# A Mamba block with a soft-tree FFN on one core: delta from eight rows of one product, and the leaf stages of the last group moved

## What is computed

```python
mod = (silu(c) @ wmod).reshape(2, 6, 1, 128)          # sa, ca, ga, sb, cb, gb; |ga|, |gb| at least 0.25
h = layernorm(x) * (1 + ca) + sa                      # x: (2, 2048, 128)
xp, z = split(h @ W_in)                               # 256 channels each
u = silu(causal_depthwise_conv(xp) + conv_b)
dt_r, Bm, Cm = split(u @ W_xp, [8, 24])               # 8, 16 and 16 columns
delta = softplus(dt_r @ W_dt + dt_bias)
h_t = exp(delta_t * A) * h_{t-1} + delta_t * B_t * u_t     # for each of 256 channels and 16 states
y_t = sum_n h_t[n] * C_t[n] + u_t * D_skip
x = x + ga * ((y * silu(z)) @ W_out)
h = layernorm(x) * (1 + cb) + sb
gate = sigmoid(h @ Wq.T @ routers.T)                  # 255 nodes of a binary tree
x = x + gb * (leaf_prob(gate) @ leaf_values @ Wout.T + Wout_b)
```

## Time and profile before

| | us |
|---|---|
| median of 3 runs | 494.55 |
| lowest, highest | 493.66, 495.66 |
| profiled execution, its own time | 495.33 |
| its span, first to last instruction | 493.5 |
| VectorE busy | 447.3 |
| GpSimd busy | 422.7 |
| TensorE busy | 406.7 |
| ScalarE busy | 378.1 |
| first scan starts | 29.64 |
| last scan ends | 471.4 |

### The profile page before, as it was taken

How to read it: one execution, slowest core, us unless ns; L and a number is a source line. 1 busy time by engine, 2 the same in 40 slices (tenths; PEclk the granted TensorE clock), 3 DMA queues, 4 the chain that set the end, 5 groups by cost and what they waited for, 6 DMA issues and landing times. The chain is left out here.

```text
span 493.5 us, 6708 instructions
## 1 busy us (share of the span) xinstructions
PE 406.7 (82%) x2133; PEld 279.7 (57%) x2164; DVE 447.3 (91%) x539; ACT 378.1 (77%) x690; POOL 422.7 (86%) x236
## 2 busy tenths in 40 slices
PE   7969665997499698997799788996899697687796
PEld 3537444675358456674558556664658455565474
DVE  6698899979999899989999889988999889999852
ACT  4478975598867898698967898698966898687715
POOL 6159899999999789998999899988999789999810
PEclk9999987997889989998999999998999989599799
DMA  6673045200830028300742027300741027300001
GB/s 168 160 298 151 1 144 222 87 0 1 301 126 27 0 42 327 108 0 2 248 149 77 2 66 303 106 2 0 259 156 60 1 62 306 107 2 21 0 1 43
DMA packets 24146, 51.06 MB, mean 103 GB/s; under 512 B 4521, under 2 KB 14256, under 8 KB 20016
## 3 DMA queue, kind: packets, MB, share of 16 engines
q1 hardware_dynamic: 24112, 50.64, 30.1%
HBM read 48.01 MB, written 2.62 MB: 103 GB/s over the span
## 5 line engine op out<-in xcount | busy, mean ns | idle before, releaser
L606 POOL TENSOR_TENSOR hc<-h,c_rows 128x1024 f32<-128x1024 f32 x127 | 298.4, 2366 | 27.0 <-DVE h L1382 26.3
L1382 DVE TENSOR_TENSOR_SCAN h<-dA,state,dbu 128x512 f32<-128x512 f32 x192 | 234.2, 1266 | 13.2 <-ACT dA L697 13.2
L697 ACT ACTIVATE dA<-delta,a_neg 128x512 f32<-128x512 f32 x256 | 173.2, 685 | 45.3 <-DVE h L1382 44.9
L1123 PE MATMUL yb<-ident,hc 128*128 128x128 f32 x1024 | 155.1, 287 | 17.8 <-POOL hc L606 16.6
L1123 PEld LDWEIGHTS yb<-ident,hc 128*128 128x128 f32 x1024 | 131.0, 149 | 64.9 <-issue 45.0
L1395 DVE TENSOR_TENSOR dbu<-du,bb 128x1024 f32<-128x1024 f32 x88 | 105.5, 1199 | 3.7 <-PE bb L1148 2.0
L593 POOL TENSOR_TENSOR dbu<-du,b_rows 128x1024 f32<-128x1024 f32 x40 | 94.6, 2364 | 4.1 <-DMA b_rows<-bc_dram 4.1
L1382 DVE TENSOR_TENSOR_SCAN h<-dA,dbu 128x512 f32<-128x512 f32 x64 | 74.2, 1205 | 5.5 <-ACT dA L697 5.4
L1023 PE MATMUL mf<-f_hT,w_conv 128*128 128x512 f32 x112 | 54.6, 612 | 2.0 <-ACT zu L757 1.4
L1148 PE MATMUL bb<-b_parts,sel 128*128 128x512 bf16 x63 | 25.1, 399 | 37.7 <-DVE dbu L1395 36.4
L1148 PEld LDWEIGHTS bb<-b_parts,sel 128*128 128x128 bf16 x88 | 8.6, 98 | 56.5 <-DVE dbu L1395 36.9
(11 more groups left out here) (206 smaller groups left out, 524.2 us busy)
## 6 DMA issues: line engine op xcount, KB each, us to landing
c_rows<-bc_dram SPq DMA_DIRECT2D x32, 1024.0 KB, 7.5
b_rows<-bc_dram SPq DMA_DIRECT2D x40, 256.0 KB, 8.9
xs<-in_L_attn_x_dram SPq DMA_DIRECT2D x8, 256.0 KB, 3.6
out_dram<-xs SPq DMA_DIRECT2D x7, 256.0 KB, 5.6
ygT<-in_L_attn_conv_w_dram SPq DMA_DIRECT2D x2, 256.0 KB, 4.3
bc_dram<-xd SPq DMA_DIRECT2D x8, 64.0 KB, 1.6
w_in<-in_L_attn_W_in_dram SPq DMA_DIRECT2D x2, 128.0 KB, 4.2
probT<-in_L_wmod_dram SPq DMA_DIRECT2D x1, 256.0 KB, 4.2
```

The costliest lines, as they stand in the source:

```text
L606: nc.gpsimd.tensor_tensor(hc[:, pair % RC, :, :], h[:, pair % RH, :, :], c_rows[:, q, n % NQ, :].unsqueeze(1).broadcast_to([P, HALVES, T]) ...
L697: nc.scalar.activation(dA[ke % RD][:, :], delta[:, ge % 2, half, :], ACT.Exp, scale=a_neg[:, half, n:n + 1]).then_inc(s_dA, 1)
L1123: last = nc.tensor.matmul(bank[:, tile], hc[:, pair % RC, half, tile], ident[:, :], start=False, stop=n == N - 1, is_transpose=True, skip_ ...
L1382: v.tensor_tensor_scan(h[:, pair % RH, half, :], dA[k % RD][:, :], dbu[:, pair % RW, half, :], start, ALU.mult, ALU.add).then_inc(s_scan, 1)
```

## The change

First, delta. The folded matrix `w_xdt`, its two transposes, two products and two copies go. W_xp's first eight columns stand in the product `xd` as rows 32 to 39 (`DT_ROW`), so `xd` gives dt, B and C in one product of two matmuls, now at steps 11 and 12. ScalarE copies it at step 13, and delta is one matmul for each half over the eight rows, at steps 14 (f) and 15 (t). Since the bank is then reused, a new product `br` at step 18 (the copy times the identity) puts `xd` back for the B parts. DRAM store and broadcast loads follow the copy.

In the first group the xd product's first half stands in front of the gate products, and four keep-warm matmuls are added, two of them while TensorE waits for the copy.

Second, the last group. Leaf stages of group 5 go to the front side's bank, at steps 4, 6 and 8 to 9 (`LAST_F`). Group 6's are `tr` 17, `node` 19 and 21, Softplus 23, `lp` 25 and 27, `ff` 29 and 30, which takes it out of `last_group`. Statistics, rstd, offset and normalisation of group 6 move from 14, 16, 16, 17 to 13, 14, 14, 15.

```diff
-              ("dt", 0): (1, (11, 12)), ("xd", 0): (1, (18, 19)), ("tr", 0): (2, (28,))},
+              ("xd", 0): (1, (11, 12)), ("dt", 0): (1, (14,)), ("br", 0): (1, (18,)), ("tr", 0): (2, (28,))},
-    ... ("dt", 1): (1, (13, 14)),
+    ... ("dt", 1): (1, (15,)),
...
-    LAST_SP = {2: -2, 25: -1}
+    LAST_F = (("lp", 0, -2, (4,)), ("lp", 1, -2, (6,)), ("ff", 0, -2, (8, 9)))
+    LAST_SP = {2: -2, 23: -1}
-    LAST_RSTD, LAST_OFF, LAST_XHAT = 16, 16, 17
+    LAST_STATS, LAST_RSTD, LAST_OFF, LAST_XHAT = 13, 14, 14, 15
...
             def dt_product(half):
-                for hh in range(HALVES):
-                    last = nc.tensor.matmul(yb[half][:, :], w_xdt[:, hh, half * P:(half + 1) * P],
-                                            zu[:, 0, HALVES + hh, :], start=hh == 0, stop=hh == HALVES - 1)
-                last.then_inc(s_dt0, 1)
+                nc.tensor.matmul(yb[half][:, :], w_dt[DT_ROW:DT_ROW + R, half * P:(half + 1) * P],
+                                 xd[DT_ROW:DT_ROW + R, :], start=True, stop=True).then_inc(s_dt0, 1)
...
                 elif name == "dt":
-                    if piece == 0:
-                        pe.wait_ge(s_silu, g + 1)
-                        if (side, g) == ("t", 1):
-                            pe.wait_ge(s_wtake, 1)
-                    last = nc.tensor.matmul(bank[:, :], w_xdt[:, piece, part * P:(part + 1) * P],
-                                            zu[:, g % 2, HALVES + piece, :],
-                                            start=piece == 0, stop=piece == HALVES - 1)
+                    wait_read(pe, "f", "xd", 0, g)
+                    if (side, g) == ("t", 1):
+                        pe.wait_ge(s_wtake, 1)
+                    last = nc.tensor.matmul(bank[:, :], w_dt[DT_ROW:DT_ROW + R, part * P:(part + 1) * P],
+                                            xd[DT_ROW:DT_ROW + R, :], start=True, stop=True)
+                elif name == "br":
+                    last = nc.tensor.matmul(bank[:, :], ident[:, :], xd[:, :], start=True, stop=True)
```

More of the change, by code:

```diff
@@ L69, in bass_adaln_mamba_tree_ffn_kernel @@
     NQ = N // QUARTERS
-    B_HI, C_ROW, B_MID, B_LO = 0, N, 64, 96
+    B_HI, C_ROW, DT_ROW, B_MID, B_LO = 0, N, 32, 64, 96
     PAIRS = K // HALVES
@@ L128, in bass_adaln_mamba_tree_ffn_kernel, with leaf_side @@
                     read_at[side].append(len(read_at[side]) + 1)
+    def leaf_side(g):
+        return "f" if g == GROUPS - 3 else "t"
     def due(name, part, g, s):
-        return [g + off for n2, p2, off, steps in jobs_of("t", g)
-                if (n2, p2, steps[-1] + 1) == (name, part, s) and ("t", name, part, g + off) in job_at]
+        side = "f" if g == LAST and name in ("lp", "ff") and any(job[0] == name and s == job[3][-1] + 1 for job in LAST_F) else "t"
+        return [g + off for n2, p2, off, steps in jobs_of(side, g)
+                if (n2, p2, steps[-1] + 1) == (name, part, s) and (side, name, part, g + off) in job_at]
     def softplus_due(g, s):
@@ L426, in _ @@
             sp.wait_ge(s_wz, 1)
-            for row, first, width in ((B_HI, R, N), (C_ROW, R + N, N), (B_MID, R, N), (B_LO, R, N)):
+            for row, first, width in ((B_HI, R, N), (C_ROW, R + N, N), (DT_ROW, 0, R), (B_MID, R, N), (B_LO, R, N)):
                 load(w_xp[:, :, row:row + width], xp_v[:, :, first:first + width], s_wxp)
@@ L901, in gate_products @@
                 last.then_inc(s_gatep, 1)
-            def dt_weight_transposes():
-                pe.wait_ge(s_wdtl, 16 * n_dt)
-                for hh in range(HALVES):
-                    last = nc.tensor.transpose(bb[0][0:R, hh * P:(hh + 1) * P], w_dtin[:, hh, :], ident[:, :])
-                last.then_inc(s_wdtt, 1)
-            def dt_weight_products():
-                pe.wait_ge(s_wdtc, 1)
-                for hh in range(HALVES):
-                    last = nc.tensor.matmul(dA[0][:, hh * DI:(hh + 1) * DI], w_dtin_t[:, hh * P:(hh + 1) * P],
-                                            w_dt[:, :], start=True, stop=True)
-                last.then_inc(s_wdtp, 1)
             def turn_x(bank, done):
@@ L961, in first_group @@
                                  skip_group_check=True).then_inc(s_r1, 1)
+                pe.wait_ge(s_wdtl, 16 * n_dt)
+                pe.wait_ge(s_modc, 1)
+                dt_product(0)
                 pe.wait_ge(s_gatec, 1)
                 dt_product(1)
+                pe.wait_ge(s_mid, 1)
+                nc.tensor.matmul(mb["f"][0][:, :], neg_ident[:, :], b_parts[:, 0, :], start=False, stop=True,
+                                 skip_group_check=True).then_inc(s_r2, 1)
                 pe.wait_ge(s_fxh, 2)
@@ L966, in first_group @@
                 turn_x(mb["t"][0], s_tr1)
-                pe.wait_ge(s_mid, 1)
-                nc.tensor.matmul(mb["f"][0][:, :], neg_ident[:, :], b_parts[:, 0, :], start=False, stop=True,
-                                 skip_group_check=True).then_inc(s_r2, 1)
             def weight_transposes(part):
@@ L1083, in product @@
                     if piece == 0:
-                        wait_read(pe, "t", "lp", 1, g)
+                        wait_read(pe, side, "lp", 1, g)
                         if g == 0:
@@ L1183, in last_group @@
                 y_sum(K - 5)
+                wait_read(pe, "f", "ff", 0, t - 2)
                 hold_rows(0)
-                product(t - 1, "t", "ff", 0, 0, 2)
                 for ks in range(K - 4, K):
@@ L1208, in last_group @@
                     last.then_inc(s_out7, 1)
-                product(t - 1, "t", "ff", 0, 1, 2)
+                keep_warm_on(dA[1], 1)
                 for i in range(2):
@@ L1413, in _ @@
                                         ALU.mult).then_inc(s_gate, 1)
-                    if tail and s == T_STATS:
+                    if tail and s == (LAST_STATS if g == LAST else T_STATS):
                         wait_read(dve, "t", "out", 0, t)
```

91 lines of the change are left out of this document (37 added, 54 removed), and 2 rows, old and new, of the table JOBS.

## The result

| | before | changed |
|---|---|---|
| median, us | 494.55 (9 runs) | 497.24 (9 runs) |
| lowest to highest | 492.86 to 495.66 | 493.84 to 498.86 |
| ratio of the changed kernel to before | | 1.0055, 95% interval 1.0029 to 1.0080 |

It is 2.7 us slower, where 2.5 us faster was forecast. The profiled execution of the changed kernel was its fastest (493.84, span 492.1); the other eight took 495.89 to 498.86.

The account below looks back on a forecast made before the run. The prediction took VectorE's scans (91% busy) as setting the pace. Start 2.0, middle 0.2 and last group 0.5 (less 3.7, plus 1.2 and 3.0) summed to 2.7 gained; against 494.55 it said 492.0 us, range 489.2 to 494.8.

Parts of the forecast that it names:

- The start, 2.0 gained: Up to the first scan: folded-matrix products gone, delta and gate instruction sooner; first scan at 27.3 instead of 29.64, 2.0 us booked.
- twice the time in low clock: Start, delta's two products: upper bound on their time, beside 0.86 us each as forecast.
- if the clock or a late transfer eats part: Start: low end of the gain, 0.7 us instead of 2.0.
- The middle, 0.2 gained: Middle groups: fewer products and xd's copy moved to step 13 without a wait; 0.2 us, between 1 lost and 1 gained.
- The last group, cost 3.7: Last group: early leaf sums and product delay yg's transpositions and the Silu block; step 13's decay at 444.3, not 440.59.
- uninterrupted work brings the clock back sooner: Last group, early leaf stages: full TensorE clock about 2 us sooner, saving about 1.9 us on the same queue.
- 1.2 back behind Softplus: Last group: group 6's Softplus at step 23 is covered by two dbu products; 1.2 of the 1.42 us stall returns.
- 3.0 back before `yg`: Last group: group 6's leaf product ends before the last sums, so the 3.48 us wait shrinks to within 0.5.
- The tail, nothing: Behind yg: the other half of group 6's leaf product and ScalarE's copy lay in waits, so removing them gains nothing.
- The low clock lasts through the early leaf stages: Rival, last group: leaf stages, transpositions and out product at half speed before the Silu block; 498 us, chance 0.08.
- The rule that the prediction took from the Trainium skill: Last group, between leaf stages: transposes do not count as TensorE work for the clock, so that stretch would lose it.
- The start does not carry: Rival, start: B's broadcast rows land when transfers allow, so only 0.7 us remains; 493.7 us, chance 0.17.

Follow-up runs that it names:

- e13: Changed kernel with the old last group, w_dt zeroed and loaded later, delta's products still over eight rows: 494.51 us, 1.0001 of the kernel before.
- e14: Changed kernel with the old last group, 128 rows in the first group's two delta products, eight in the other fourteen: 490.94 us, 0.9926 of before.
- e4: Changed kernel with five keep-warm matmuls instead of one between output product and last normalised rows' transpositions: 496.61 us, 1.0030 of before.
- e7: Changed kernel with group 5's leaf stages at steps 12, 14 and 16 to 17 instead of 4, 6 and 8 to 9: 492.65 us, 0.9956 of before.
- e10: Changed kernel with the old last group, all delta products over 128 rows, w_dt zero-padded and loaded later: 493.15 us, 0.9960 of before.
- e5: Changed kernel with the old last group and seven keep-warm matmuls instead of two during the wait for xd's copy: 494.13 us, 0.9992 of before.
- e6: Changed kernel with seven keep-warm matmuls instead of two while TensorE waits for xd's copy: 495.12 us, 1.0019 of before.
- e12: Changed kernel with group 5's leaf stages at 12, 14, 16 to 17 and seven keep-warm matmuls at the start: 492.36 us, 0.9959 of before.

## Why the prediction was wrong

**The start, 2.0 gained: the term was right and did not reach the end.** First scan forecast 27.3; ten profiles with eight rows have 27.02 to 28.44 (mean 27.8), the four with the old delta 29.54 to 30.58 (mean 30.0): 2.2 sooner. Its parts held: the gate TENSOR_SCALAR alone at 0.43, delta's products at the price of full ones. What failed is "I book 2.0 us", that a first scan started sooner is a kernel ended sooner. In nine of the ten the clock then stood at 1.2 GHz for 6.8 to 10.2 us, and 27.4 to 27.8 us passed to the Silu scan instead of 24.1 to 25.8. The low clock at the start had a place only as a bound ("twice the time in low clock" for delta's products, 0.7 "if the clock or a late transfer eats part"), and always on the way to the first scan; what TensorE does behind it, the z products and B fills, had no term. By e13 and e14 the cause is the eight-row form, which I had priced by its duration alone. Why a product over eight rows lets the clock fall, no run shows.

**The middle, 0.2 gained:** nothing; 372.3 to 372.6 in all but two profiles, both of the old delta (373.45, 373.94). The stalls behind the two table blocks are unchanged (1.53 behind Silu, 1.45 behind Softplus), ScalarE does not wait at the copy of `xd`.

**The last group, cost 3.7:** measured 3.1 to 4.4. Right in size and place: the sums at low clock in front of `yg` (2.05 and 1.91 for the first), the product in front of the fills. The gap before the scan of step 13 came as several stalls, not one. The hope that uninterrupted work brings the clock back sooner came true (426.4 in the first profile against 432.2 before), and the cost came all the same.

**The last group, 1.2 back behind Softplus:** 1.43 to 0.30, right.

**The last group, 3.0 back before `yg`: this is the mis-sized term.** It was read from 3.48 in the earlier trace rows as if every execution had it. The low clock that went with it, seen in the earlier trace rows, was that execution's; in before's second profile the wait is 1.50, and it becomes 1.06, so 0.44 comes back and not 3.0. With it the last group's sum is 3.7 - 1.1 - 0.4 = 2.2 lost, where I had 0.5 gained. Those 2.7 alone turn 492.0 into 494.7; the start's 2.0 that do not arrive bring it to 496.7, and the measured time is 497.24.

**The tail, nothing:** half wrong. All seven profiles with the old last group have 17.42 to 17.51 behind `yg`; of eleven with the new one and one keep-warm matmul, six have 18.5 to 18.6, and these six have a stretch of 3.4 us at 1.2 GHz between `yg` and the end, which the other five lack until their last microsecond. In the changed kernel's first profile:

```profile
477.57 0.38 PE L875 MATMUL dA<-idle 128*128 128x512 bf16 x1
479.22 0.44 PE L870 MATMUL yb<-ident,t_xhat 128*128 128x128 f32 x2 [1.27 <-DVE t_xhat L1422]
...
480.38 3.21 PE L1199 MATMUL dA<-t_hT,w_node 128*128 128x256 f32 x8
```

and in the kernel before:

```profile
480.17 1.06 PE L1091 MATMUL mt<-leaf_out_g,probT 128*128 128x128 f32 x8
481.82 0.44 PE L874 MATMUL yb<-ident,t_xhat 128*128 128x128 f32 x2 [0.59 <-DVE t_xhat L1446]
...
482.99 1.99 PE L1218 MATMUL dA<-t_hT,w_node 128*128 128x256 f32 x8
```

The half leaf product (1.06) that stood in this gap is gone, TensorE's clock fell (0.83 and 0.60 from 479 to 485) and a product that took 1.99 takes 3.21. I had said the pieces "lay in waits: nothing". They did, but they were also work on TensorE. That this is why the clock falls is argued, not shown: five of the eleven kept their clock without the product, and e4 did not decide it.

**The rivals.** "The low clock lasts through the early leaf stages", 498, is nearest in number and not in mechanism: the clock was back at 426.4 in the first profile and 431.6 in the second, before the first transposition. The rule that the prediction took from the Trainium skill, TensorE: Matmul & The Clock Gate, Part 4: PE-mode transpose, would have had the transposes behind the leaf stages lose the clock. In the changed kernel it was indeed low from 447 to 454:

```profile
448.67 0.61 PE L1130 MATMUL bb<-b_parts,sel 128*128 128x512 bf16 x1 [5.58 <-DVE dbu L1371]
```

But TensorE had stood idle for 5.58 us before; in e7 the same transposes, with the leaf stages between, stood in windows at 1.00. The idle time is enough to explain it without the rule, though no run sets the two apart, and VectorE did not wait for it. "The start does not carry" had the right outcome for another reason than the one given.

## What to carry to other kernels

A term read from one profiled execution must be checked for what the clock happened to be there: a wait whose releaser ran at half speed is a sample, not a cost, and a second profile of the same kernel showed as much (1.50 for 3.48). A start won on the path to the first scan counts only once TensorE's work behind it has been followed to the next wait that the change leaves in place. When a small product is moved in front of others on an engine that runs in order, count who is queued behind it; the same three leaf stages cost 3 to 4 us at steps 4 to 9 and nothing at 12 to 17.

## What the runs showed of the hardware

- A 512-column fp32 product over 8 rows took as long as one over 128 (1.98 and 1.88 for two), but with the eight-row form TensorE's granted clock was lower: 0.904 to 0.92 over the kernel in all eleven profiles that have it in the middle groups, 0.947 to 0.962 in the four with 128 rows throughout. Two such products at the start cost 3.6 us by the medians of e14 (five executions) and e13; with 128 rows everywhere (e10) it was 1.4. Padding with zero rows cost no time in the product.
- Filling a gap of 1.07 us on TensorE with matmuls did not keep the clock with eight rows: it fell 5 to 6 us later in e5 and e6, and at the same 26.6 us in e12 as in e7.
- Executions of one kernel differ by where the clock falls: the stretch to the Silu scan took 24.10 and 25.80 us in the two profiles of the kernel before, 24.32 and 27.81 in the two of the changed one, whose tail took 18.62 and 17.50. Times of one kernel stand in steps: with e10 five executions at 490.3 to 491.0 and six at 493.1 to 493.6. That the clock makes these steps too is not shown; only one of the twelve was profiled.
